# One move of the software pipeline in a fused attention and state-space kernel: the next item's front half shifted, the softplus minimum on ScalarE, GpSimd's products three steps ahead

## The reference, cut to what matters

```python
xn = layer_norm(x)                        # over the 512 channels, per pixel
chunks = xn split into 4 groups of 128 channels        # 4 sequences of length 4096 per image
xi, z = split(in_proj(chunk))             # 128 -> 256 + 256
xc = silu(causal_conv4(xi) + conv_b)
dt, B, C = x_proj(xc)                     # 8 + 16 + 16 rows
dt = softplus(dt_proj(dt) + dt_b)
h[s] = exp(dt * A[s]) * h[s] + (dt * xc) * B[s]        # 16 states s, recurrent over the pixels
y = sum_s h[s] * C[s] + xc * D
y = out_proj(y * silu(z)) + skip * chunk
out = x + proj(layer_norm(y))
```

## Time and profile before

| | |
|---|---|
| median of 3 runs | 18126.95 us (18125.56 to 18134.58) |
| the profiled execution | 18123.12 us, its span 18121.3 us |
| busy: POOL | 15765.8 us (87%) |
| busy: DVE | 15022.4 us (83%) |
| busy: PE | 14746.6 us (81%) |
| busy: ACT | 10780.9 us (59%) |
| mean granted PE clock | 0.92 of full |

### The profile page before, as it was taken

One profiled execution on the slowest core, in us unless ns is written; L12 is line 12 of the kernel. 1 busy time (PEld: TensorE's weight loads), 2 busy tenths in 40 slices (PEclk: granted clock), 3 DMA queues, 4 the chain that ended last, 5 costly groups with the idle time before them and its releaser, 6 DMA issues.

```text
span 18121.3 us, 159160 instructions
## 1 busy us (share of the span) xinstructions
PE 14746.6 (81%) x30720; PEld 5850.1 (32%) x30720; DVE 15022.4 (83%) x13131; ACT 10780.9 (59%) x18036; POOL 15765.8 (87%) x6524
## 2 busy tenths in 40 slices
PE   6888878888788887888878888788887888878887
PEld 2333333333333333333333333333333333333333
DVE  7888868888688886888868888688886888868888
ACT  4666646665466664666546665466654666556665
POOL 5999969999699996999969999699996999969998
PEclk8999989999899998999989999899998999989999
DMA  3444434444344443444434444344443444434443
GB/s 131 143 148 151 148 110 142 149 151 148 111 142 149 150 147 111 144 149 149 147 111 144 149 148 147 113 144 148 148 147 113 145 147 149 146 113 144 145 147 131
DMA packets 739067, 2535.98 MB, mean 140 GB/s; under 512 B 77240, under 2 KB 78016, under 8 KB 721728
## 3 DMA queue, kind: packets, MB, share of 16 engines
q1 hardware_dynamic: 738112, 2527.45, 41.3%
HBM read 2376.15 MB, written 150.99 MB: 139 GB/s over the span
## 4 chain that ended last, share of the span: by engine, by line
PE 36%; issue 24%; DVE 19%; POOL 15%; ACT 5%; DVEq 1%; DMA 0%; POOLq 0%; ACTq 0%
PE FL L365 18%; PE YP L365 18%; DVE RING L887 11%; POOL RING L1171 6%; POOL RING L1158 4%; DVE RING L868 3%; POOL ITEM L1185 2%; POOL ITEM L1181 2%; DVE YZ L893 1%; POOL ITEM L1176 1%; DVE LV L913 1%; ACT DA L626 1%; DVE ST L933 1%; ACT LS L714 1%; ACT EM L656 1%
## 5 line engine op out<-in xcount | busy, mean ns | idle before, releaser
L887 DVE TENSOR_TENSOR_SCAN RING<-DA,HS,RING 128x512 f32<-128x512 f32 x8192 | 9977.5, 1264 | 1480.8 <-ACT DA L626 1088.3
L1171 POOL TENSOR_TENSOR RING<-RING,CS 128x1024 f32<-128x1024 f32 x4096 | 9938.0, 2439 | 1110.3 <-DVE RING L887 1100.7
L365 PE MATMUL YP<-RING,EYE 128*128 128x512 f32 x16384 | 8443.1, 645 | 1677.7 <-POOL RING L1171 1676.8
L626 ACT ACTIVATE DA<-ITEM,AN 128x512 f32<-128x512 f32 x8192 | 5559.0, 687 | 5159.9 <-DVE RING L887 5146.3
L365 PEld LDWEIGHTS YP<-RING,EYE 128*128 128x128 f32 x16384 | 3191.1, 203 | 6624.8 <-issue 3705.9
L1158 POOL TENSOR_TENSOR RING<-ITEM,BS 128x1024 f32<-128x1024 f32 x1536 | 3734.3, 2431 | 1.1
L868 DVE TENSOR_TENSOR RING<-DTP,BS 128x1024 f32<-128x1024 f32 x2560 | 3083.0, 1204 | 322.9 <-issue 256.2
L365 PE MATMUL FL<-XN,WC 128*128 128x512 f32 x4096 | 1886.3, 604 | 94.6 <-ACT XN L704 83.2
L1176 POOL TENSOR_TENSOR ITEM<-ITEM,EX 128x1024 f32<-128x1024 f32 x256 | 601.0, 2348 | 1046.3 <-ACT EX L673 1046.3
L365 PE MATMUL FL<-LS,WP 128*128 128x512 f32 x2048 | 1071.2, 659 | 319.4 <-DVE YB L899 270.6
L365 PEld LDWEIGHTS FL<-XN,WC 128*128 128x128 f32 x4096 | 792.3, 195 | 1152.0 <-issue 1011.8
(11 more groups left out here) (119 smaller groups left out, 10121.3 us busy)
## 6 DMA issues: line engine op xcount, KB each, us to landing
BS<-bc_rows SPq DMA_DIRECT2D x2048, 512.0 KB, 4.9
CS<-bc_rows SPq DMA_DIRECT2D x2048, 512.0 KB, 3.5
XR<-in_x SPq DMA_DIRECT2D x128, 1024.0 KB, 7.3
x_slices<-XR SPq DMA_DIRECT2D x64, 1024.0 KB, 8.0
XR<-x_slices SPq DMA_DIRECT2D x64, 1024.0 KB, 7.4
out<-XR SPq DMA_DIRECT2D x64, 1024.0 KB, 7.8
ITEM<-in_wqkv SPq DMA_DIRECT2D x24, 1024.0 KB, 5.6
bc_rows<-ROWS SPq DMA_DIRECT2D x256, 64.0 KB, 4.5
```

The costliest lines, as they stand in the source:

```text
L365: return pe.matmul(*a, **k)
L626: act.activation(DA[:, h, :], DT[:, i % 2, h, :], ACT.Exp, scale=AN[:, h, s:s + 1]).then_inc(dA_ready, 1)
L887: dve.tensor_tensor_scan(H[:, slot(n), h, :], DA[:, h, :], U[:, slot(n), h, :], HS[:, i % ITEMS, h, s:s + 1], ALU.mult, ALU.add).then_inc( ...
L1171: pool.tensor_tensor(G[:, slot(n)], H[:, slot(n)], CS[:, s % C_ROWS, :].unsqueeze(1).broadcast_to([P, NH, T]), ALU.mult).then_inc(g_ready, 1)
```

## The change

Nothing is left out of the computation, and no tile size or ring changes. The order written out by hand does, in these parts.

- **GpSimd's products.** `POOL_U` becomes (0, 1, 2, 7, 8, 9) instead of (0, 1, 3, 5, 7, 9), still six, and POOL makes them three steps ahead instead of two. DVE's ten are placed by a table: U3 in step 2, U4 and U5 in step 3, U6 in step 4, U10 to U15 in steps 8 to 13. In j = 3 (`late`) U5 moves to step 4 and the front half lies one step later.
- **Convolution.** The first half (`xi_first`) of the item after next is issued in step 15 of the item before, the second half (`xi_second`) in step 0 behind the sum of step 14.
- **Silus** in step 3 instead of 4, DVE's gate staying in step 2; the rest of the front half moves up a step too; out_proj from step 7 or 9 to step 4, and the D matmuls from the head of the item to step 9.
- **Softplus minimum.** DVE's `min` goes; ACT computes the same from |v| by a relu and an exp, in place.
- **Scratch.** The cubic's scratch is YZ instead of DTX. The reciprocal deviation of the first norm is written to PSUM (LP) instead of the SBUF tile RS, and `scale_norm` reads it there.

```diff
-POOL_U = (0, 1, 3, 5, 7, 9)
+POOL_U = (0, 1, 2, 7, 8, 9)
+U_LEAD = 3
+AHEAD = ((), (), (3,), (4, 5), (6,), (), (), (), (10,), (11,), (12,), (13,), (14,), (15,), (), ())
+AHEAD_LATE = ((), (), (3,), (4,), (5, 6), (), (), (), (10,), (11,), (12,), (13,), (14,), (15,), (), ())
...
-                if s == 0:
-                    if not first:
-                        pe.wait_ge(yz_ready, tile * ITEMS + i)
-                    for h in range(NH):
-                        mm(YP[:, h, :], DD[:, h, :], XC[:, i % 2, h, :], start=True, stop=False)
+                if s == 0 and not first:
+                    pe.wait_ge(yz_ready, tile * ITEMS + i)
...
+                    if s < 2 and not first:
+                        state_sum(tile, n - 2)
                     if front:
-                        if s == 0:
+                        if s == 0 and d:
                             front_left(tile, w)
-                            pe.wait_ge(xn_ready, tile * ITEMS + w + 2)
-                            xi_half(tile, w + 1, 0)
...
+                            xi_first(tile, w + 1)
+                        if s == d:
+                            xi_second(tile, w, first, ln2)
...
+                    if front and s == NS - 1 and j != 2:
+                        front_left(tile, w + 1)
+                        xi_first(tile, w + 2)
...
-                act.activation(EM[:, :, :], EM[:, :, :], ACT.Exp, scale=-1.0).then_inc(e_ready, 1)
+                act.activation(EX[:, :, :], EM[:, :, :], ACT.Exp, scale=-1.0).then_inc(e_ready, 1)
+
+            def dt_small(tile, i):
+
+                act.activation(EM[:, :, :], EM[:, :, :], ACT.Relu, bias=LOGSMALL[:, 0:1]).then_inc(capped, 1)
+                act.wait_ge(capped, tile * ITEMS + i + 1)
+                act.activation(EM[:, :, :], EM[:, :, :], ACT.Exp, scale=-1.0,
+                               bias=LOGSMALL[:, 0:1]).then_inc(small_ready, 1)
...
-                        if s == 4:
+                        if s == 3 + d:
                             if not first:
                                 act.wait_ge(yz_ready, tile * ITEMS + w)
                             silus(tile, w + 1)
...
-            def make_ahead(tile, n, first=False, front=True):
-
-                if front or (n + 2) // NS == n // NS:
-                    make_u(tile, n + 2, first=first)
+            def make_ahead(tile, n, j, first=False):
+
+                s = n % NS
+                for m in (AHEAD_LATE if late(j) else AHEAD)[s]:
+                    make_u(tile, n - s + m, first=first)
...
-            def dt_small(tile, i):
-                dve.wait_ge(excess_ready, tile * ITEMS + i + 1)
-                dve.tensor_scalar(EM[:, :, :], EM[:, :, :], SMALL, None, ALU.min).then_inc(small_ready, 1)
-
...
-                dve.tensor_tensor(LV[:, :, :], LV[:, :, :], RS[:, :].unsqueeze(1).broadcast_to([P, NCH, T]),
+                dve.tensor_tensor(LV[:, :, :], LV[:, :, :], LP[:, :].unsqueeze(1).broadcast_to([P, NCH, T]),
                                   ALU.mult).then_inc(scaled1, 1)
...
-                    if (n + 2) % NS in POOL_U and (front or s < NS - 2):
-                        make_u(tile, n + 2, first=first)
+                    if (n + U_LEAD) % NS in POOL_U and (front or s < NS - U_LEAD):
+                        make_u(tile, n + U_LEAD, first=first)
```

More of the change, by code:

```diff
@@ L431, in front_left, with xi_first, xi_second @@
                 pe.wait_ge(relu_ready, tile * (2 * ITEMS) + 2 * i + 2)
+            def xi_first(tile, i):
+                pe.wait_ge(xn_ready, tile * ITEMS + i + 1)
+                xi_half(tile, i, 0)
+            def xi_second(tile, w, first, ln2):
+                j = w % ITEMS
+                ahead = tile + w // ITEMS
+                if j in (0, 2) and not first:
+                    pe.wait_ge(yb_ready, tile * ITEMS + w - 1)
+                if j == 1 and ln2:
+                    pe.wait_ge(log2_ready, ahead)
+                if j == 2 and ln2:
+                    pe.wait_ge(final_ready, (ahead - 1) * NCH + NCH)
+                if j == 3:
+                    pe.wait_ge(scaled1, ahead + 2)
+                xi_half(tile, w + 1, 1)
             def window(tile, w, first=False, front=True, ln1=True, ln2=True):
                 j = w % ITEMS
+                d = late(j)
                 ahead = tile + w // ITEMS
@@ L472, in window @@
                         if s == 6:
-                            pe.wait_ge(log2_ready, ahead)
                             pe.wait_ge(yn_ready, ahead)
+                            pe.wait_ge(yb_ready, tile * ITEMS + w)
                             proj(0, (0, 1))
@@ L507, in window @@
                             channel_mean(LS, var1_ready, (2, 3))
-                    if s == out_step(j) and not first:
-                        out_proj(tile, w - 1)
-                    if s > 1 or not first:
+                    if front and s == NS - 1 and j != 2:
+                        front_left(tile, w + 1)
+                        xi_first(tile, w + 2)
+                    if s > 1:
                         state_sum(tile, n - 2, first=first and s == 2)
-                    if j == 1 and ln2 and s == NS - 1:
-                        pe.wait_ge(final_ready, (ahead - 1) * NCH + NCH)
             def attention(b):
@@ L573, in first_front @@
                 dt_proj(tile, 0, 1)
+                front_left(tile, 0)
+                xi_first(tile, 1)
             def last_end(tile):
@@ L719, in rstd @@
                 act.wait_ge(log, v)
-                act.activation(RS[:, :], RS[:, :], ACT.Exp, scale=-0.5).then_inc(done, 1)
+                act.activation(dst, RS[:, :], ACT.Exp, scale=-0.5).then_inc(done, 1)
             def window(tile, w, first=False, front=True, ln1=True, ln2=True):
                 j = w % ITEMS
+                d = late(j)
                 ahead = tile + w // ITEMS
@@ L820, in first_front @@
                 dt_exp(tile, 0)
+                dt_small(tile, 0)
                 dt_excess(tile, 0)
@@ L1220, in _ @@
                 dt_x(b * NT, 0)
-                make_u(b * NT, 0, first=True)
-                make_u(b * NT, 1, first=True)
+                for n in range(U_LEAD):
+                    if n in POOL_U:
+                        make_u(b * NT, n, first=True)
                 window(b * NT, 0, 0, first=True)
```

132 lines of the change are left out of this document (65 added, 67 removed).

## The result

The changed kernel takes 17516.22 us (median of 4 runs, 17513.09 to 17534.64) against 18129.76 us of the kernel before (4 runs, 18125.56 to 18134.58): a ratio of 0.9664, 95% interval 0.9647 to 0.9680. It is faster by 614 us. The forecast was 17158 us, 969 less than before.

The account below looks back on a forecast made before the run. POOL's work, its starvation by DVE, and fills and drains were taken as the bound. 15540 work + 350 in-loop idle + (1046 + 17) fills + 175 image ends + 24 gave 17152 span, forecast 17158 us; range 16850 to 17600.

Parts of the forecast that it names:

- rival 2: New waits: moved waits, such as PE's convolution or the dtx copy, reach POOL; 650 to 850 us idle, 17450 to 17650; 15%.
- the prediction's own sign of being wrong: Wrong if POOL's busy time stays at 15766 or G still waits over 600 us, most likely at G3 or G10.
- the 58% forecast: The prediction's main case: a time of 16950 to 17450 us, given a 58% chance.
- rival 1: POOL saturates: DVE's slack also swallows the j = 3 waits, idle near 30 us, 16830 us in all; chance 12%.
- rival 4: Slower: PE at half clock at the seam makes G3 8 us late; 1580 us idle, 18380; decides from 210 us; 5%.
- POOL's own work: POOL's busy time falls from 15765.8 to 15540 us: 131 from scale_norm reading PSUM, 95 from min leaving DVE.
- this stays: The G after the cubic's last step still takes 3.34 instead of 2.35 us, both cubic inputs being in SBUF as before.
- In-loop idle: POOL's waiting ahead of G inside the loop falls from 1110 to 350 us: 5 us a tile, 320, plus 30.
- j = 3: Item with DVE's statistics and silus a step later: step 10 reaches POOL about 3.6 us late.
- j = 0: First item of a tile: POOL wants step 3 at 6.9 us, gets it at 8.3, so idles 1.4 us.
- The silus: Silus from 3.7 to 8.3 us, DA of step 4 at 9.0, DVE needs it at 9.4: 2.72 us stall covered.
- ACT: Relu and exp replacing min add 560 us on ACT, hidden in the loop; +17 us at the fills.

Follow-up runs that it names:

- the same test in the kernel before: Kernel before the change, with the cubic's last step reading PSUM tile DTP times 0 instead of SBUF scratch, cubic's value left out: 17920.91 us.
- The experiments with the statistics: Next image's statistics moved within j = 3 of the changed kernel: 17528.96 us; row and block sums moved to j = 1, cubic from PSUM everywhere: 17118.22 us.
- the first experiment: Changed kernel with the cubic's last step reading PSUM tile DTP times 0 instead of SBUF tile YZ, cubic's value left out: 17201.55 us.
- four moves of instructions: Changed kernel, each alone: j = 1 cubic to step 11, 17507.99 us; statistics within j = 3, 17528.96; DVE products off silus, 17515.39; dt x copy later, 17526.21.
- a fifth: Kernel with the cubic from PSUM everywhere, plus DVE's row and block sums of the next image moved from j = 3 to j = 1: 17118.22 us.

## Why the prediction was right, and where its size was wrong

**Right.** The direction and the range held. The time lies above the forecast's own 16950 to 17450, in the stretch of rival 2, and the prediction's own sign of being wrong came true: G waits 670.6 us, over the 600 named, and G10 is the largest single place. So the range held by its width, and not because the 58% forecast was right. What the bound is was right: POOL's work, its waits for DVE, fills and ends of images are the time, before and after, to within some 30 us. Two of its numbers do not fit its own working: 16850 to 17600 is not quite from rival 1 (16830) to the upper edge of rival 2 (17650), and in rival 4 the 210 us are reached when 88% of the items have the stretch, not 80%.

**POOL's own work**, 15540 forecast, 15442.7 measured. The two gains are there: no U takes 4.4 us any more (56 did), no G 2.7 (some 248 did), and with `scale_norm` back on SBUF POOL has 129.5 us more work. What was not foreseen is that the cubic lengthens a POOL instruction by 1.0 us more rarely now, 129 times instead of 248; where it is shut out until POOL stops, none is lengthened. The step "this stays" was wrong there, to POOL's advantage in busy time and not in total.

**In-loop idle**, 350 forecast, 817 measured. This is the term that failed. In parts:
- *"Its inputs, now YZ and EM, are both in SBUF as before, so this stays".* It does not stay. 276 us of the 817 lie behind the cubic, and the cubic from PSUM in its place gives back 319 us of the time, against 210 from the same test in the kernel before. The prediction took the 1.0 us of one row as the price. That row was from a POOL which had idled ahead of G just before. Sorted by the POOL instruction in which the cubic is issued, without the fills: before, 248 of 248 in `dt_first`, 1.8 to 2.4 us each. After, 176 in `dt_first` (119 of 1.7 to 3.0 us, 57 of 4.1 to 5.3) and 72 in a G (10 of 1.7 to 1.8, 20 of 6.4 to 8.1, 42 of 8.2 to 8.8). What decides between them is told below the list.
- *j = 3*, 230 us forecast for its 64 items, 376 measured. G10 was named, at 3.6 us an item; it waits 2.8 (177 us in 63 waits). G4, 130 us, was not: the prediction let DVE come into an item with all the lead that U2 allows, ending the scans of step 2 at 0.1 us after G0 begins. In the trace they end at 0.5 in j = 0 and at 2.1 in j = 3 (medians). The experiments with the statistics show that moving them within j = 3 brings nothing and moving a part of them out of it does.
- *j = 0*, G3: 1.4 us forecast, 1.8 measured (114 us in 64 waits). The hand-written item was close: its scans of step 3 end at 8.5 us, forecast 8.3. Its cause, the gate behind PE's sum 15, is argued from DVE's wait of 423 us for PE; no run tested it, and G3 takes up some of what is freed elsewhere (187 us in the first experiment).
- *The silus.* DVE's wait for DA fell from 1088 to 537 us, but the cover by DVE's own products was not what mattered (taken away, no difference); the lead of three steps was (225 us). DVE's wait for U, "gone" by the prediction, is 256.5 us.

**When the cubic gets in.** The instruction in which it is issued is not what decides; how long POOL had run without a pause goes with it. Counted is how many instructions POOL had started since it last paused (over 0.02 us) when it came to the one in which the cubic was issued:

```
instructions since POOL's last pause      0 or 1     9 or 10    21 or more
kernel before: issued, got in at once    248, 248       -            -
changed kernel: issued, got in at once    90, 90     80, 39       78, 0
```

"At once" is at the end of the POOL instruction in which the cubic was issued. The 119 others got in only when POOL stopped at a wait, none at an end in between. In the kernel before, the changed one and the seven experiments that keep the cubic on two SBUF inputs (in one of them only in j = 1) and `min` on ACT it is 861 of 861 with 0 or 1, 294 of 605 with 8 to 11, and 0 of 582 with 12 or more. With `min` back on DVE, where it is itself held up by POOL a few instructions earlier, 76 of 76 got in after 9 or 10; that a turn of DVE counts like a pause of POOL would explain it, and is not shown. So the collision is dear where POOL's run without a pause is long, and the change made those runs longer.

**ACT**: 560 us forecast, 584 measured (L688 and L690); ACT's busy time rose by 467. At the fills +17 us were forecast. There are 8 waits of together 1045.3 us now. Before, the 64 waits of 1046.3 us held 56 short ones inside the loop, of together 18 us by the timeline, so that the fills had 1028. The +17 are right.

**The rivals.** Saturation did not come. Slower did not come: the mean granted clock was 0.929, against 0.92 before, and in j = 0 the scans of step 3 end 0.2 us after the forecast, where rival 4 has G3 8 us late. New waits did, for a reason that rival 2 did not name.

**Open.** What decides 8 to 11 instructions after a pause was not settled: of cubics issued 0.4 us into `dt_first` in j = 0, some got in behind it and some only one product later. The long runs of POOL come with certain items and places of the order, and no run varied the length of a run alone.

## What to carry to other kernels

A collision costs more once the gaps of the other engine are gone (210 us before the change, 315 after): when a change saturates an engine, price again everything that shares a port with it, and take the price in the rows of the loose schedule as a lower bound. Ask of every shortened or lengthened instruction on the second engine where that engine's lead is spent next: a product moved away from the silus or a copy a step later made no difference where there was slack, while 1.2 us more of `scale_norm`, once a tile, came with 127 us more of POOL's idle time ahead of G. And try the cheap test, one input in PSUM, before rearranging an order by hand: it brought 315 us here, as against nothing from four moves of instructions and 79 us from a fifth.

## What the runs showed of the hardware that was not expected

A VectorE instruction of 1.2 us with both inputs in SBUF stood 8.45 us behind GpSimd, across three ends of GpSimd instructions that followed each other without a wait; with one of its inputs in PSUM it took 1.20 us at the same place. The Trainium skill ("SBUF — State Buffer", Summary: rules for kernel authors) says that when a VectorE instruction has two SBUF inputs and the GpSimd one reads SBUF, the second one to issue "**fully blocks** until the first finishes". The trace agrees that it is blocked and does not share, but "until the first finishes" is too short: the wait was over at the end of that first instruction in 248 of 248 cases when GpSimd had paused at most one instruction earlier, and in none of 78 after 21 or more instructions without a pause; there it lasted until GpSimd itself stopped. When VectorE does get in, the GpSimd instruction behind it takes 3.3 us instead of 2.3. The single-input `tensor_scalar` went from 671 ns in the kernel before to 2824 ns beside the denser GpSimd; the same page (section Who interferes with whom) counts `tensor_scalar` among those that can take the shared pair, and these numbers agree.
